# Stacks of split products: a dimension's six rows side by side instead of six blocks of sixteen rows

## The reference, cut to what matters

```python
def attend(qx, kx, vx):
    scores = jnp.einsum('bhqd,bhkd->bhqk', qx, kx) * scale
    return jnp.einsum('bhqk,bhkd->bhqd', jax.nn.softmax(scores, axis=-1), vx)
# blocks of 64 tokens; a block of queries meets the first, the last and three neighbouring blocks of
# keys; the first and the last block of queries meet all of them
...
def _forward(x, ...):                       # layer norm, dense branch, top 2 of 8 experts,
    abel_out = _gelu(xn @ abel_w + abel_b)  # three rotations by expm, a gate between the branches
    h = _gelu(jnp.einsum('bsd,edh->ebsh', xn, ew1) + eb1[:, None, None, :])
    eo = jnp.einsum('ebsh,ehd->ebsd', h, ew2) + eb2[:, None, None, :]
...
x = x + _layernorm(attention(_layernorm(x)))
x = x + _layernorm(ffn(_layernorm(x)))
```

## Time and profile before

| | |
|---|---|
| median of 3 executions | 1994.57 us |
| lowest and highest | 1987.76 and 1997.65 us |
| the profiled execution, its own time | 2002.51 us |
| its span | 2000.7 us |
| TensorE busy | 1591.1 us (80%) |
| VectorE busy | 1223.5 us (61%) |
| ScalarE busy | 928.4 us (46%) |
| GpSimd busy | 707.2 us (35%) |
| TensorE clock granted, mean | 0.941 of full speed |
| fetches of the stacks (w<-split_spill) | 384, 128 KB each |

### The profile page before, as it was taken

One profiled execution on the slowest core, in us unless ns is written; L12 is line 12 of the kernel. 1 busy time (PEld: TensorE's weight loads), 2 busy tenths in 40 slices (PEclk: granted clock), 3 DMA queues, 4 the chain that ended last, 5 costly groups with the idle time before them and its releaser, 6 DMA issues. The chain is left out here.

```text
span 2000.7 us, 35686 instructions
## 1 busy us (share of the span) xinstructions
PE 1591.1 (80%) x10365; PEld 1075.6 (54%) x10430; DVE 1223.5 (61%) x3633; ACT 928.4 (46%) x1788; POOL 707.2 (35%) x716
## 2 busy tenths in 40 slices
PE   3878888887887887887888887747999999999800
PEld 2534444444444444444444444536888888888700
DVE  6746765765765765765756755333565656565367
ACT  1045655655655655655656657412333333333234
POOL 1011223413413413314324313432445444444457
PEclk9889999999999998999999999978999999999955
DMA  3453256256265355364365351564665665566477
GB/s 118 78 107 83 55 124 134 82 126 144 72 127 118 89 137 112 81 146 105 90 148 101 82 138 66 167 204 104 139 137 97 142 135 113 123 135 119 49 257 253
DMA packets 185576, 241.78 MB, mean 121 GB/s; under 512 B 24584, under 2 KB 156048, under 8 KB 185296
## 3 DMA queue, kind: packets, MB, share of 16 engines
q1 hardware_dynamic: 158544, 203.58, 40.2%
q0 software_dynamic: 26880, 36.33, 10.9%
HBM read 133.40 MB, written 105.91 MB: 120 GB/s over the span
## 5 line engine op out<-in xcount | busy, mean ns | idle before, releaser
L956 ACT ACTIVATE pexp<-scT 128x512 f32<-128x512 f32 x768 | 440.6, 599 | 366.0 <-PE scT L743 323.7
L1126 DVE TENSOR_REDUCE mx<-work 128x1 f32<-128x320 f32 (+2 forms) x1024 | 493.3, 549 | 60.1 <-PE work L723 57.8
L1600 POOL DMA_INDIRECT y_rows<-rows_add,row_of x144 | 227.0, 1576 | 294.6 <-DMA y_rows<-rows_add,row_of 210.0
L723 PE MATMUL work<-w 126*128 126x320 bf16 (+4 forms) x1280 | 268.0, 302 | 60.3 <-DVE mx L1126 26.6
L743 PE MATMUL scT<-w 128*128 128x192 bf16 (+3 forms) x1472 | 258.8, 274 | 62.8 <-ACT pexp L956 56.9
L1632 PE MATMUL h_ps<-inT,w1c 128*128 128x256 f32 x1152 | 262.1, 381 | 2.4 <-DVE inT L1684 2.4
L1645 PE MATMUL o_ps<-w,hT 128*128 x1152 | 260.4, 379 | 0.0
L1632 PEld LDWEIGHTS h_ps<-inT,w1c 128*128 128x128 f32 x1152 | 219.7, 191 | 33.1 <-issue 3.1
L743 PEld LDWEIGHTS scT<-w 128*128 128x128 bf16 x1536 | 125.6, 98 | 205.4 <-ACT pexp L956 141.6
L1575 ACT ACTIVATE rows_add<-rows_out,row_share 128x257 f32<-128x257 f32 x144 | 65.6, 503 | 355.2 <-DVE rows_out L1700 256.5
L1645 PEld LDWEIGHTS o_ps<-w,hT 128*128 128x128 f32 x1152 | 213.4, 190 | 26.1
(11 more groups left out here) (173 smaller groups left out, 2172.2 us busy)
## 6 DMA issues: line engine op xcount, KB each, us to landing
w<-split_spill SPq DMA_DIRECT2D x384, 128.0 KB, 5.9
split_spill<-split SPq DMA_DIRECT2D x64, 384.0 KB, 4.7
rows_in<-z_rows SPq DMA_DIRECT2D x72, 265.0 KB, 4.7
y_rows<-pre SPq DMA_DIRECT2D x16, 514.0 KB, 6.6
y<-y_rows SPq DMA_DIRECT2D x16, 514.0 KB, 6.1
x_rows<-x SPq DMA_DIRECT2D x16, 512.0 KB, 2.7
abel_rows<-pre SPq DMA_DIRECT2D x16, 512.0 KB, 5.5
abel_in<-abel_rows SPq DMA_DIRECT2D x16, 512.0 KB, 4.5
```

Of the source, the lines that this page charges most:

```text
L723: ins = nc.tensor.matmul(work[t][:, at:at + hi - lo], tile(qst[par][0:K_SCORE, h, :], t), kst[par][0:K_SCORE, h, lo:hi], start=True, stop= ...
L956: nc.scalar.activation(pexp[:, (q * GROUP + n) % NPB, :], scT[n % 2][:, :], ACT.Exp, scale=DH ** -0.5).then_inc(s_exp, 1)
L1126: nc.vector.reduce_max(mx[:, c:c + 1], work[t][:, 0:n], AX_X).then_inc(w_free[t], 1)
L1600: pool.indirect_dma_start(kept.y_rows, bass.IndirectOffsetOnAxis(ap=row_of[n][:, r:r + 1], axis=0), rows_add[n % 2][:, r, :], None, comput ...
```

## The change

The six rows of one dimension stand side by side: row 6d + g holds dimension d of group g, where it was row 16g + d. `MASK_ROW` is 96 and `NGRP` is 6, so each fetch writes partitions g, g + 6, up to g + 90. Both stacks are filled by the same line. Number, order, size and source of the DMAs, the waits and every other instruction stay as they are.

```diff
                 for g, part in enumerate(parts):
                     src = spill[par, m].rearrange("(h d) s c -> d h s c", d=DH)[:, :, part, :]
-                    sp.dma_start(st[par][g * DH:(g + 1) * DH, 8 * half:8 * half + 8, :], src)\
+
+                    sp.dma_start(st[par][g:MASK_ROW:NGRP, 8 * half:8 * half + 8, :], src)\
                       .then_inc(s_stack[half], 16)
```

## The result

| | before | after |
|---|---|---|
| median of 20 executions | 1997.8 us | 1990.02 us |
| lowest and highest | 1987.76 and 2004.22 us | 1980.93 and 1997.64 us |
| the profiled execution, its own time | 2002.51 us | 1987.4 us |
| its span | 2000.7 us | 1985.6 us |

The ratio is 0.9961 with a 95% interval of 0.9948 to 0.9974. That is 7.8 us faster, 5 to 10 us by the interval. The forecast had been 7.4 us.

The account below looks back on a forecast made before the run. TensorE was taken to be bound by slowly written stack fetches in steps 1 and 2 only. Waits of 5.8 us plus 1.65 us of clock gave 7.4 us, so 1994.57 became 1987.2 us, range 1980 to 1998 us.

Parts of the forecast that it names:

- The two places: TensorE's first matmul of the maxima in steps 1 and 2: waits of 3.33 + 2.46 = 5.8 us go.
- Writing limits the fetches, not reading: Stacks' fetches: writing 16 neighbouring partitions slows packets to 123 ns; spread out, half 0 lands some 4 us earlier.
- Rival A: Stacks' fetches: slow packets come from the source, so new partitions change nothing, 1994.6 us; chance 17%.
- The issue: SyncE's issue of the fetches stays at 432 ns each with the partition step of six: 0 us.
- The pace: Writing of the fetches rises from 135 runs per us to well above 200, at most 280.
- The clock: Behind the waits of steps 1 and 2, falls to 1.2 GHz go: 1.65 us, from 0 up to 4.4 us.
- B: All steps: lighter fetch load or fewer clock falls give about 1 us in each of 13 more, 1974 us; 10%.
- C: Fetches crowd puts and neighbouring fetches, half 0 lands later, steps 1, 2 and the 13 others lose, 2016 us; 7%.
- D: Steps 1 and 2: the wait goes but VectorE holds them up later, gain down to 0, 1994.6 us; 6%.

Follow-up runs that it names:

- the complement: The changed kernel with old rows in batches 1 and 2 and new rows in the 14 others: 0.9994 of the kernel before.
- the second profile of the changed kernel: Profile of the changed kernel run once more with no edit, beside the kernel before on one chip: 0.9935 of the kernel before.
- put 2 behind: The changed kernel with put 2 issued behind restack 1 instead of ahead of it: 0.9931 of the kernel before, and again 0.9931.
- the two complementary kernels: New rows in batches 1 and 2 alone, 0.9943 of the kernel before; new rows everywhere but there, 0.9994.

## Why the prediction was right, point by point

**The two places.** Right. Two batches of sixteen carry the gain (0.9943 against 0.9994 for the complement), as the view of waits had said with its count of 2. The size is less settled: 7.8 us in the 20 runs of the result, but 11 to 13 us for the two kernels with the new rows in these batches beside one another, where the whole kernel had more time at 2.4 GHz than the two places explain.

**Writing limits the fetches, not reading.** Right. With the same source in the same order, a packet went from 123 to 51 ns and the landing from 5.9 to 2.9 us. Rival A asked for a landing that stays, and it fell. The argument had rested on the first fetch of a step being fast. The groups in another order showed it from the other side: the same fetches of the same source, slower by which destinations follow each other.

**The issue.** This term was mis-sized. I took 0 us and allowed for 100 ns more on each, since no row had a partition step other than one. It was 168 ns: 12 x 0.168 = 2.0 us on the last fetch of half 0. I also wrote that faster writing would take that up. It took up most of it: of 5.8 us of waiting 1.8 were left, where I had written 0 to 0.5. So the waits gave 4.0 us, not 5.3 to 5.8.

**The pace.** I had put "well above 200" runs per us. It was 197, the pace of the issue. So the 213 per us and the 75 ns, which I had worked out by the rule of the Trainium skill (SBUF — State Buffer, Door 1: The DMA port swizzle), were not put to the test: the mean was 51 ns a packet, with the engines waiting for SyncE.

**The clock.** Mis-sized to the other side. The way from step 1 to 2 became 68.5 - 65.2 = 3.3 us shorter, of which the wait of step 2 is 2.0; from 2 to 3 it became 66.9 - 65.1 = 1.8 us shorter, and no wait for the stacks is in that. So 1.3 + 1.8 = 3.1 us are left for the clock where I had counted 1.65, the two groups of 24 matmuls alone. It is inside the bound of 4.4 us from the windows. The falls from 2.4 to 1.2 GHz are gone even though a wait of 0.5 to 1.4 us remained. I had called them falls behind the waits, but they began within them: the mean granted clock is already 0.69 and 0.57 in the last us of the two waits of the kernel before.

The 3.1 us take it that a wait costs all of its time, which isn't quite so. From step 2 to step 3 it is 64.5 us in the second profile of the changed kernel, with a wait of 1.51 us in step 2, and 65.3 us in both profiles with put 2 behind, with waits of 0.24 and 0.25 us, all at 2.4 GHz throughout. So some 0.8 us of that wait were made up for at once. The clock may have given that much more, and the waits that much less; the sum stays.

**Sum.** 4.0 + 3.1 = 7.1 us in the profiles up to step 3, where 5.8 + 1.65 = 7.4 had been written: two errors of about the same size and opposite sign. The time was right for partly wrong sizes. Four other profiles with the old rows in steps 1 and 2 show waits of 7.1 to 8.6 us there instead of 5.8 (without the two whose edit lengthens or covers this wait), so the profile on which the forecast rests was at the small end.

**The rivals.** A fell. B, with a gain in every step, was what the single pair of profiles seemed to show (15.1 us in the span), and the load of the fetches as its cause fell with the two complementary kernels. Its other half, fewer falls of the clock in later steps, is just what that pair has (51 against 27 us at 1.2 GHz), and the other profiles show it as chance. For the timed runs with 11 and 13 us it stays open. C did not come: the landing is 2.5 to 5.6 us over all steps. But its mechanism is real. The order of groups made the fetches crowd each other more, steps 3 and 11 began to wait, and the kernel became 0.24% slower. D came in part at most, with the 0.8 us of a wait that were made up for.

## What to carry to other kernels

A transfer that is hidden nearly everywhere still has a price where its cover is thinnest. Look at each place with its own cover, not at the mean, and price also the clock behind a wait. Before you believe that an edit helps in all rounds of a loop, do it in the rounds that wait and in all the others, as two kernels; a single pair of profiles differed by 10 us in steps that the edit didn't help. Sum up the time at each level of the clock before you compare two profiles: here that explained the 10 us. And when a DMA's shape changes, the issue is part of the price. Once it was what ended last, the order of issue counted (waits from 1.8 and 2.3 us to 0.2 and 0.4), which had shown no effect before.

## What the runs showed of the hardware

- The issue of a 128 KB DMA from SyncE took 600 ns with a partition step of two or six, and 431 ns with a step of one. A put of 384 KB, the same in all kernels, took 0.59 us behind six such DMAs and 0.43 us behind six with a step of one (steps 1 to 3).
- Fetches of runs of 1 KB into 16 neighbouring partitions went at 133 to 135 runs per us when the next DMA wrote the 16 partitions above, or in an order with steps of 48 and 64. They went at 117 in the order that puts 0 to 15 next to 32 to 47, and 16 to 31 next to 48 to 63. Spread six partitions apart they kept up with the issue, 197 per us, at 51 ns a packet.
- The crowding doesn't show on the first fetch after a pause. Its packets take 54 ns, and only those behind it take 123 ns.
- All twelve waits of TensorE for the stacks of 2.9 us or more came with a fall of the granted clock to 1.2 GHz, which often began within the wait. None of 1.5 us or less did. Of the five between, those of 1.65 and 2.46 us did, and those of 1.69, 2.08 and 2.58 us didn't. Behind the wait of 1.85 us for the last maxima of step 1 the clock fell in one profile of the changed kernel and not in the other.
- Steps 3 to 15 took 894 us with 24 us at 1.2 GHz and 905 us with 51.
